# Attention's work on TensorE in four blocks a batch by how it uses the array, with the other engines' order redrawn

## The chip, the cores and the metric

The kernel runs on one core of one Trainium2 chip. The metric is the device time of one execution in microseconds; several executions give a median. The core has five engines that matter here, each of which works through its own list of instructions in order and waits for others at semaphores: TensorE (PE in the profile), VectorE (DVE), ScalarE (ACT), GpSimd (POOL) and SyncE (SP, which only issues transfers).

## The reference, cut to what matters

2048 tokens (8 batches of 256) with 128 features go through two layers, each of them a mixing part and a feed-forward part, with a residual and a layer norm behind each. The change touches only the third part, a linear attention with exponential feature maps:

```python
qkv = x @ Wqkv + bqkv                       # 16 heads of 8
def _feature_map(t, omega):                 # 32 features a head
    return jnp.exp(einsum('bhnd,dm->bhnm', t, omega) - 0.5 * sum(t * t, -1))
k_sum = jnp.sum(k_prime, axis=2)
denominator = einsum('bhnm,bhm->bhn', q_prime, k_sum)[..., None]
k_v = einsum('bhnm,bhnd->bhmd', k_prime, v)
numerator = einsum('bhnm,bhmd->bhnd', q_prime, k_v)
out = numerator / (denominator + 1e-06)
return out @ Wout + bout
# around it: x = _layernorm(x + attention(x))
```

(The reference calls it with four batches of 512 in mind, but here its input has eight batches of 256.) Ahead of it stand a gated convolution and a mixture of eight experts, behind it a gated MLP with two square layers.

## The kernel before, in words

Every engine's list is written out by hand. In attention each engine works in steps `s`; `attention(step, first, end)` calls `attention_step(s)` for each. One call handles several batches at once, at different stages: `values(s - 2)` is batch `s - 2`, and a call for a batch that doesn't exist does nothing. Semaphores count up by batch; `wait(engine, sem, n)` waits only where `n > 0`. A batch `b` goes through these stages:

- GpSimd `answers_sum` (L603) and `x2_residual` (L609) add the experts' two answers and the kept row. For batches 4 to 7 the answers come from HBM late. VectorE `x2_moments` (L962, L970) takes mean and variance, GpSimd `x2_root` (L477, L480) the inverse root, VectorE `x2_norm` (L987) normalises.
- TensorE `x2_transposes` (L1990) turns the rows; ScalarE `turned_x2` copies them out twice; GpSimd `low_x2` (L616) makes the low part.
- TensorE `keys_or_queries(b, 0)` makes keys, `(b, 1)` queries (three products each, L1695 to L1697); ScalarE `biased_and_squared` writes them and their squares. TensorE `values` (L2001), VectorE `biased_v` (L1483).
- TensorE `key_features` (L2026) and then, in the same PSUM room, `query_features` (L2035); ScalarE `key_exps` (L831) and `query_exps` (L837).
- TensorE `key_sums` (L2048); VectorE `own_sums` (L1492, L1495) transposes and masks them; TensorE `query_products` (L2065, L2062) makes numerator and denominator.
- VectorE `inverse_sums` (L1504, a reciprocal) and `attended` (L1510); TensorE `attention_rows` (L2076, L2077); VectorE `x3_residual` (L1517) and `x3_moments`; GpSimd `x3_root`; VectorE `x3_norm` (L987); TensorE `x3_transposes` (L2086); ScalarE `high_x3` and VectorE `low_x3` (L1532) split it for the MLP.

TensorE addresses its array in three ways here, which the profile shows as contraction rows * output columns: the full array (128*128: transposes, keys, queries, values, rows out), 32 rows (32*128: the two feature maps, four products side by side) and 32 columns (128*32: key sums and query products, again four side by side). The step of before goes through them as values | query features | x2 transposes, queries | key sums | key features | rows out, x3 transposes, keys | query products: seven changes a step.

VectorE's step in before, in order, is `biased_v(s-3)`, `inverse_sums(s-5)`, `attended(s-5)`, `own_sums(s-4)`, `x3_norm(s-6)`, `x3_residual(s-5)`, `x2_moments(s)`, `x2_norm(s-1)`, `low_x3(s-6)`, `x3_moments(s-5)`. `x3_residual(b)` waits for `attention_rows(b)`; `values(b)` waits for the transpose in `own_sums(b-2)`, which frees its half of PSUM bank 2. After the last step VectorE goes on with the MLP's gating (L1554).

## Time and profile before

| | us |
|---|---|
| median of 3 runs | 332.81 |
| lowest, highest | 332.07, 333.74 |
| span of the profiled execution | 343.1 |
| TensorE busy | 313.5 (91%) |
| VectorE busy | 249.8 (73%) |
| ScalarE busy | 189.2 (55%) |
| GpSimd busy | 161.4 (47%) |

The profiled execution is 10.3 us longer than the median: the times of the rows are those of that execution, and a difference worked out from them is set against its 343.1. Busy is the time in which an engine has an instruction under way. Consecutive instructions overlap at their ends, so that what an instruction costs in a full engine is read from its start to the next one's start, not from its duration. The chain that ended last runs 54% on TensorE and 14% on VectorE over the whole span. Attention lies between about 185 and 243 us.

### The profile page before, as it was taken

What the parts mean: (1) busy time and instruction counts of PE and PEld (TensorE: products, weight loads), DVE (VectorE), ACT (ScalarE), POOL (GpSimd) and SP (SyncE); (2) the same over time, 40 slices, a digit from 0 to 9 for tenths busy, and PEclk for the clock granted to TensorE, in tenths of its full rate; (3) what the DMA queues carried; (4) which work ended last, traced back from release to release, by engine and by line L of the source; (5) the groups of instructions that cost most, each with busy time, mean ns of one, the idle gap of its engine ahead of it and who ended that gap; (6) DMA issues with size and microseconds to landing.
All of it is one profiled execution on the core that took longest, in us unless ns stands there. A gap on an engine that the chain in (4) does not pass through costs nothing.

```text
span 343.1 us, 8922 instructions
## 1 busy us (share of the span) xinstructions
PE 313.5 (91%) x2917; PEld 283.8 (83%) x2917; DVE 249.8 (73%) x852; ACT 189.2 (55%) x401; POOL 161.4 (47%) x221
## 2 busy tenths in 40 slices
PE   7999999988893699999999999999889999999993
PEld 4988988978782599999888776776678999999993
DVE  2577988878890348968985589878995787667844
ACT  3144886654450246646547655654657766767333
POOL 1014577867777445698588584221130433144200
PEclk9999999999998589999999999999999999999998
DMA  6991011122133432522430400000000000000001
GB/s 207 418 403 67 16 34 33 33 54 48 49 71 93 152 111 71 186 63 65 115 96 32 129 14 2 2 3 4 1 2 0 3 15 18 15 15 0 16 18 34
DMA packets 17051, 23.22 MB, mean 68 GB/s; under 512 B 3440, under 2 KB 14448, under 8 KB 16224
## 3 DMA queue, kind: packets, MB, share of 16 engines
q1 hardware_dynamic: 14016, 17.84, 16.3%
q0 software_dynamic: 2272, 4.69, 4.1%
q8 instruction: 24, 0.39, 0.5%
q10 hardware_dynamic: 720, 0.14, 0.2%
q14 instruction: 19, 0.16, 0.1%
HBM read 16.93 MB, written 6.73 MB: 69 GB/s over the span
## 4 chain that ended last, share of the span: by engine, by line
PE 54%; DVE 14%; another core or an unknown queue 4%; issue 4%; ACT 3%; POOL 2%; DVEq 0%; POOLq 0%; ACTq 0%
PE ps L2104 9%; PE ps L2105 9%; PE ps L1931 6%; PE ps L1695 3%; PE ps L1697 3%; PE ps L1917 3%; PE ps L2168 3%; PE ps L1696 3%; PE ps L2026 3%; PE ps L2035 2%; PE ps L2048 2%; PE ps L2065 1%; DVE sb_work L1504 1%; PE ps L1891 1%
## 5 line engine op out<-in xcount | busy, mean ns | idle before, releaser
L2104 PE MATMUL ps<-sb_w_hi,sb_fh_hi 128*128 128x256 f32 x256 | 61.2, 283 | 1.2 <-DVE sb_w_lo L957 0.6
L2105 PE MATMUL ps<-sb_w_lo,sb_fh_hi 128*128 128x256 f32 x256 | 59.9, 278 | 0.0
L2104 PEld LDWEIGHTS ps<-sb_w_hi,sb_fh_hi 128*128 128x128 f32 x256 | 48.2, 188 | 2.4 <-issue 1.1
L2105 PEld LDWEIGHTS ps<-sb_w_lo,sb_fh_hi 128*128 128x128 f32 x256 | 48.2, 188 | 0.0
L1931 PE MATMUL ps<-sb_w,sb_stage 128*128 x234 | 34.6, 286 | 4.6 <-issue 4.6
L493 POOL DMA_INDIRECT routed<-sb_rows_of,sb_row x32 | 32.0, 999 | 11.8 <-issue 8.7
L1931 PEld LDWEIGHTS ps<-sb_w,sb_stage 128*128 128x128 f32 x234 | 30.9, 201 | 5.0 <-issue 4.8
L643 POOL TENSOR_TENSOR sb_w_lo<-sb_x_in,sb_w_hi 128x256 fp32r<-128x256 f32 x24 | 17.5, 754 | 34.9 <-DVE sb_w_hi L1627 34.9
L477 POOL TENSOR_TENSOR sb_veps_h<-sb_mv_h,sb_eps 128x2 f32<-128x2 f32 x16 | 5.1, 318 | 54.5 <-DVE sb_mv_h L970 48.9
L1695 PE MATMUL ps<-sb_w_hi,sb_rT_hi 128*128 x78 | 29.3, 375 | 0.4 <-ACT sb_stage L771 0.4
L595 POOL DMA_INDIRECT answers<-sb_stage x24 | 24.1, 1004 | 11.0 <-ACT sb_stage L777 7.1
L1697 PE MATMUL ps<-sb_w_hi,sb_rT_lo 128*128 x78 | 25.9, 332 | 0.0
L1696 PE MATMUL ps<-sb_w_lo,sb_rT_hi 128*128 x78 | 25.8, 330 | 0.0
L1917 PE MATMUL ps<-sb_const,sb_stage 128*128 128x128 f32 x117 | 20.1, 281 | 4.3 <-ACT sb_stage L783 3.1
L1695 PE MATMUL ps<-sb_front_hi,sb_xT_hi 128*128 128x512 f32 (+1 forms) x64 | 23.2, 362 | 0.7 <-DVE sb_xT_lo L1004 0.7
L595 POOL DMA_INDIRECT answers<-sb_xT_in x15 | 14.4, 960 | 13.9 <-ACT sb_xT_in L777 9.0
L882 ACT ACTIVATE sb_xT_in<-ps,sb_ff_s 128x256 f32<-128x256 f32 x32 | 14.5, 474 | 11.5 <-PE ps L2105 9.0
L874 ACT ACTIVATE sb_work<-ps,sb_ff_s 128x256 f32<-128x256 f32 x32 | 13.9, 474 | 12.5 <-PE ps L2105 12.5
L1696 PE MATMUL ps<-sb_front_lo,sb_xT_hi 128*128 128x512 f32 (+1 forms) x64 | 20.5, 320 | 0.0
L1697 PE MATMUL ps<-sb_front_hi,sb_xT_lo 128*128 128x512 f32 (+1 forms) x64 | 20.5, 320 | 0.0
L1917 PEld LDWEIGHTS ps<-sb_const,sb_stage 128*128 128x128 f32 x117 | 14.6, 144 | 6.3 <-issue 4.0
L891 ACT ACTIVATE sb_x_in<-ps,sb_ff_s 128x256 f32<-128x256 f32 x32 | 14.2, 477 | 9.3 <-PE ps L2105 9.3
(307 smaller groups left out, 928.6 us busy)
## 6 DMA issues: line engine op xcount, KB each, us to landing
sb_stage<-in_w SPq DMA_DIRECT2D x2, 1408.0 KB, 13.9
sb_stage<-routed SPq DMA_DIRECT2D x24, 65.0 KB
sb_w<-in_w SPq DMA_DIRECT2D x1, 1536.0 KB, 18.6
sb_x_in<-in_x_tok SPq DMA_DIRECT2D x1, 1024.0 KB, 9.6
sb_x_in<-in_ff_h SPq DMA_DIRECT2D x1, 1024.0 KB
sb_xT_in<-in_ff_h SPq DMA_DIRECT2D x1, 1024.0 KB
sb_got_first<-answers SPq DMA_DIRECT2D x4, 256.0 KB, 3.4
sb_w<-answers SPq DMA_DIRECT2D x4, 256.0 KB, 4.1
```

The lines of the kernel that those rows point to most:

```text
L493: nc.gpsimd.indirect_dma_start(routed[:, :], bass.IndirectOffsetOnAxis(ap=row[:, b, r:r + 1], axis=0), rows_of[:, b, r, :], None).then_inc ...
L595: nc.gpsimd.indirect_dma_start(answers[:, :], bass.IndirectOffsetOnAxis(ap=routed_row(t)[:, AT_DEST:AT_DEST + 1].bitcast(u32), axis=0), ro ...
L643: nc.gpsimd.tensor_tensor(a_lo[:, m, :], f_a[:, m, :], a_hi[:, m, :].bitcast(fp32), ALU.subtract).then_inc(ff["a_lo"], 1)
L882: nc.scalar.activation(f_last[:, m, :], half_bank(6, m), ACT.Gelu, scale=ff_s[:, 3, m:m + 1]).then_inc(ff["g2"], 1)
L891: nc.scalar.activation(f_g[:, m, :], second_bank(b, m), ACT.Gelu, scale=ff_s[:, 2, m:m + 1]).then_inc(ff["g1"], 1)
L1695: mm(dst, lhs[0], rhs[0], start=start, stop=False)
L1696: mm(dst, lhs[0], rhs[1], start=False, stop=False)
L1697: return mm(dst, lhs[1], rhs[0], start=False, stop=stop)
L1917: last = transpose(ps[:, 1, k * P:(k + 1) * P], hid[:, u % FLY, k * P:(k + 1) * P], ident)
L1931: last = mm(ps[:, down_bank(u), 0:D], hidT[:, u % FLY, k * P:(k + 1) * P], w2[:, e, k, :], start=k == 0, stop=k == HIDDEN_TILES - 1)
L2104: mm(dst, w_hi, x_hi, start=start, stop=False)
L2105: last = mm(dst, w_hi, x_lo, start=False, stop=stop and exact)
```

## The change

TensorE's step is put in the order key features (32 rows) | keys, queries, values, x2 transposes, rows out, x3 transposes (full array) | query features (32 rows) | query products, key sums (32 columns): four changes a step. Keys and queries of a batch stand behind each other and wait for both of the batch before. The queries' exponentials get a second buffer, `qp_of`, in room that the experts' part has left free, so that they wait for the query products of two batches before. The `attention_step` of ScalarE, VectorE and GpSimd is written anew to this order, and one batch more of the work before the features is in flight. The work itself, its instructions and their sizes, stay as they are.

```diff
-        qp = act1_room[:, 0:HEAD_GROUPS * SEQ].rearrange("p (g t) -> p g t", t=SEQ)
+        qp_of = [r[:, 0:HEAD_GROUPS * SEQ].rearrange("p (g t) -> p g t", t=SEQ) for r in (act1_room, hid_room)]
 # GpSimd
             def attention_step(s):
-                answers_sum(s)
-                x3_root(s - 6)
-                x2_root(s - 1)
-                low_x2(s - 2)
-                x2_residual(s)
+                answers_sum(s + 1)
+                x2_residual(s + 1)
+                x3_root(s - 4)
+                low_x2(s)
+                x2_root(s + 1)
...
                 x2_root(3)
-                answers_sum(4)
-                x2_residual(4)
-                low_x2(3)
-                x2_root(4)
-                answers_sum(5)
-                x2_residual(5)
...
-            attention(attention_step, first=6, end=ATTENTION_STEPS + 1)
+            attention(attention_step, first=3, end=ATTENTION_STEPS - 1)
 # ScalarE
-                    act.wait_ge(at["qk"], 2 * b + part + 1)
+                    act.wait_ge(at["qk"], 2 * b + (part + 1 if b == 0 else 2))
...
-                    wait(act, at["nd"], b)
-                    nc.scalar.activation(qp[:, :, :], features, ACT.Exp).then_inc(at["qp"], 1)
+                    wait(act, at["nd"], b - 1)
+                    nc.scalar.activation(qp_of[b % 2], features, ACT.Exp).then_inc(at["qp"], 1)
...
                     act.wait_ge(at["tr"], b + 1)
+                    wait(act, at["tr3"], b - 4)
...
             def attention_step(s):
-                query_exps(s - 3)
-                turned_x2(s - 1)
-                biased_and_squared(s - 2, 1)
                 key_exps(s - 2)
+                biased_and_squared(s - 1, 0)
+                turned_x2(s)
                 high_x3(s - 5)
-                biased_and_squared(s - 1, 0)
+                query_exps(s - 2)
+                biased_and_squared(s - 1, 1)
...
-            attention(attention_step, first=4, end=ATTENTION_STEPS - 1)
+            attention(attention_step, first=2, end=ATTENTION_STEPS - 1)
 # VectorE
             def attention_step(s):
-                biased_v(s - 3)
-                inverse_sums(s - 5)
-                attended(s - 5)
-                own_sums(s - 4)
-                x3_norm(s - 6)
-                if s < ATTENTION_STEPS:
-                    x3_residual(s - 5)
-                x2_moments(s)
-                x2_norm(s - 1)
-                if s < ATTENTION_STEPS:
-                    low_x3(s - 6)
-                    x3_moments(s - 5)
+                own_sums(s - 3)
+                x2_norm(s)
+                biased_v(s - 1)
+                x3_residual(s - 4)
+                x3_moments(s - 4)
+                x2_moments(s + 1)
+                low_x3(s - 5)
+                x3_norm(s - 4)
+                inverse_sums(s - 3)
+                attended(s - 3)
...
-            attention(attention_step, first=6, end=ATTENTION_STEPS + 1)
+            attention(attention_step, first=3, end=ATTENTION_STEPS - 1)
 # TensorE
-                    wait(pe, at["x3_lo"], b - 4)
+                    wait(pe, at["x3_lo"], b - 5)
...
-                    wait(pe, at["st"], 2 * b + part)
+                    wait(pe, at["st"], 2 * b)
...
             def attention_step(s):
-                values(s - 2)
-                query_features(s - 3)
-                x2_transposes(s - 1)
-                keys_or_queries(s - 2, 1)
-                key_sums(s - 3)
                 key_features(s - 2)
+                keys_or_queries(s - 1, 0)
+                keys_or_queries(s - 1, 1)
+                values(s - 1)
+                x2_transposes(s)
                 attention_rows(s - 4)
                 x3_transposes(s - 5)
-                keys_or_queries(s - 1, 0)
+                query_features(s - 2)
                 query_products(s - 3)
+                key_sums(s - 2)
...
             keys_or_queries(1, 0)
+            keys_or_queries(1, 1)
             values(1)
+            x2_transposes(2)
             query_features(0)
-            x2_transposes(2)
-            keys_or_queries(1, 1)
             odd_weights()
             key_sums(0)
-            key_features(1)
-            keys_or_queries(2, 0)
-            query_products(0)
-            attention(attention_step, first=4, end=ATTENTION_STEPS - 1)
+            attention(attention_step, first=3, end=ATTENTION_STEPS - 1)
```

The calls that ScalarE and VectorE made by hand ahead of their steps for the same batches go away with it.

## Rows read from the trace of the kernel before

**Rows 1.** Busy time by stretch: us, then busy us (instructions) by engine; attention's stretch

```profile
185.00:243.00 58.00, 54.94 (x939) 40.99 (x940) 46.24 (x139) 34.42 (x65) 24.79 (x42) 1.00 0.08 24
```

**Rows 2.** Timeline of TensorE, one steady step: start us, us, engine, line, instructions

```profile
216.11 0.71 PE L2001 MATMUL ps<-sb_wv,sb_work 128*128 128x128 f32 x4
216.75 1.15 PE L2035 MATMUL ps<-sb_x_in,sb_omega 32*128 32x256 f32 x16
217.83 0.44 PE L1990 MATMUL ps<-sb_const,sb_rows_of 128*128 128x128 f32 x2
218.03 0.36 PE L1695 MATMUL ps<-sb_xT_hi,sb_qk_hi 128*128 128x256 f32 x1
...
218.55 1.08 PE L2048 MATMUL ps<-sb_stage,sb_xT_in 128*32 128x128 f32 x32
219.56 1.17 PE L2026 MATMUL ps<-sb_omega,sb_x_in 32*128 32x128 f32 x32
220.67 0.23 PE L2076 MATMUL ps<-sb_bout,sb_ones_bf 128*128 128x128 bf16 x1
...
222.12 0.64 PE L2065 MATMUL ps<-sb_stage,sb_hT 128*32 128x256 f32 x8
...
223.22 0.71 PE L2001 MATMUL ps<-sb_wv,sb_work 128*128 128x128 f32 x4
```

**Rows 3.** Timeline of TensorE before the steady steps, values behind a full-array product

```profile
186.56 0.61 PE L2001 MATMUL ps<-sb_wv,sb_work 128*128 128x128 f32 x4
```

**Rows 4.** Timeline of VectorE over the steady step

```profile
216.33 0.48 DVE L962 BATCH_NORM_STATS2 sb_stats_h<-sb_stage 128x6 f32<-128x128 f32 x2
...
217.12 0.46 DVE L1483 TENSOR_TENSOR sb_xT_in<-ps,sb_bv 128x128 f32<-128x128 f32 x2
217.50 1.75 DVE L1504 RECIPROCAL sb_work<-ps 128x256 f32<-128x256 f32 x1
219.28 0.42 DVE L1510 TENSOR_TENSOR sb_work<-ps,sb_work 128x256 f32<-128x256 f32 x1
219.70 0.45 DVE L1492 STREAM_TRANSPOSE sb_hT<-ps 128x256 f32<-128x256 f32 x1
220.18 0.31 DVE L1495 TENSOR_TENSOR sb_hT<-sb_hT,sb_const 128x128 f32<-128x128 f32 x1
220.42 0.60 DVE L987 SCALAR_TENSOR_TENSOR sb_rows_of<-sb_stage,sb_mv_h,sb_rstd_hs 128x128 f32<-128x128 f32 x2
221.54 0.42 DVE L1517 TENSOR_TENSOR sb_stage<-ps,sb_rows_of 128x256 f32<-128x256 f32 x1 [0.52 <-PE ps L2077]
221.88 0.60 DVE L987 SCALAR_TENSOR_TENSOR sb_rows_of<-sb_work,sb_mv_odd,sb_rstd_odd 128x128 f32<-128x128 f32 x2
222.41 0.42 DVE L1532 TENSOR_TENSOR sb_w_lo<-ps,sb_w_hi 128x256 fp32r<-128x256 f32 x1
```

**Rows 5.** Timeline of GpSimd over the steady step

```profile
217.29 0.19 POOL L477 TENSOR_TENSOR sb_veps_h<-sb_mv_h,sb_eps 128x2 f32<-128x2 f32 x1 [3.47 <-DVE sb_mv_h L970]
217.56 0.71 POOL L480 TENSOR_TENSOR sb_rstd_hs<-sb_veps_h,sb_minus_half 128x2 f32<-128x2 f32 x1
...
219.62 0.73 POOL L616 TENSOR_TENSOR sb_xT_lo<-sb_work,sb_xT_hi 128x256 fp32r<-128x256 f32 x1 [0.41 <-ACT sb_work L846]
```

**Rows 6.** Timeline of GpSimd, the two sums of batch 4

```profile
195.34 0.73 POOL L603 TENSOR_TENSOR sb_work<-sb_w 128x256 f32<-128x256 f32 x1 [3.21 <-DMA sb_w<-answers]
196.14 0.73 POOL L609 TENSOR_TENSOR sb_res<-sb_work,sb_rows_of 128x256 f32<-128x256 f32 x1
```

**Rows 7.** The reciprocals' line: durations ns min/median/max, first and last start

```profile
L1504 DVE RECIPROCAL sb_work<-ps x8: 1726/1748/1757, 194.9 to 242.9; 128x256 f32<-128x256 f32 x8
```

**Rows 8.** Timeline of VectorE, the first product of the MLP's gating

```profile
245.54 0.87 DVE L1554 SCALAR_TENSOR_TENSOR sb_x_in<-ps,sb_ff_s,sb_work 128x256 f32<-128x256 f32 x2
```

**Rows 9.** Timeline of VectorE, the product over GpSimd's addition

```profile
205.12 0.83 DVE L1495 TENSOR_TENSOR sb_hT<-sb_hT,sb_const 128x128 f32<-128x128 f32 x1
```

**Rows 10.** Timeline of GpSimd, that addition

```profile
205.07 0.73 POOL L609 TENSOR_TENSOR sb_res<-sb_work,sb_rows_of 128x256 f32<-128x256 f32 x1
```

More of the change, by code:

```diff
@@ L910, in _ @@
             biased_and_squared(0, 1)
-            key_exps(0)
-            biased_and_squared(1, 0)
-            query_exps(0)
-            turned_x2(2)
-            biased_and_squared(1, 1)
-            key_exps(1)
-            biased_and_squared(2, 0)
-            attention(attention_step, first=4, end=ATTENTION_STEPS - 1)
+            attention(attention_step, first=2, end=ATTENTION_STEPS - 1)
             nc.scalar.activation(touched[:, :], ones[:, 0:1], ACT.Silu)
@@ L1652, in _ @@
             odd_count()
-            own_sums(0)
-            x2_norm(3)
-            biased_v(2)
-            inverse_sums(0)
-            attended(0)
-            x2_moments(4)
-            own_sums(1)
-            x3_residual(0)
-            x2_norm(4)
-            x2_moments(5)
-            x3_moments(0)
-            attention(attention_step, first=6, end=ATTENTION_STEPS + 1)
+            attention(attention_step, first=3, end=ATTENTION_STEPS - 1)
             mlp_first(0, (0, 1))
@@ L2065, in query_products @@
                             last = mm(ps[32 * g:32 * g + 32, 3, a * SEQ:(a + 1) * SEQ], sums,
-                                      qp[:, g, :], start=a == 0, stop=True)
+                                      qp_of[b % 2][:, g, :], start=a == 0, stop=True)
                     last.then_inc(at["nd"], 1)
```

## Prediction, made before the changed kernel was run

> **What bounds the kernel now.** I read the page's slices for the stages, then busy time by stretch, then the timeline of each engine over one steady step of attention. In attention TensorE is busy 54.9 of 58.0 us and VectorE 46.2 [rows 1]. The reader should then see that a steady step lasts 223.22 - 216.11 = 7.11 us, from one `values` to the next, and that TensorE has no hole in it [rows 2]. In the same step VectorE once waits for TensorE, 0.52 us before `x3_residual` [rows 4]. So TensorE's own order sets the pace, and VectorE is close behind. How close is the question of this change, since it both shortens TensorE's step and redraws VectorE's.
>
> **TensorE's own step.** Seven changes of array shape become four. What one costs is seen in the same four products `values`: 0.71 us behind query products of 128*32 [rows 2], 0.61 behind full-array products [rows 3], so 0.1 within the group; the drain ahead of the group is not isolated by any row, and I bound it by 0 and 0.1 more. Three changes fewer are 0.3 to 0.6 us a step, so TensorE's step would be 6.5 to 6.8 us. I take 6.65. The TensorEngine Tiling page of the Trainium skill (Tiling Modes, Key Properties) says that changing the mode drains the engine, which these rows bear out in direction.
>
> **VectorE's own step.** From start to start [rows 4]: reciprocal 1.78 (217.50 to 219.28), `attended` 0.42, `own_sums` 0.72 (219.70 to 220.42), a norm 0.53 (221.88 to 222.41) twice, `x3_residual` 0.34, moments 0.79 (216.33 to 217.12) twice, `biased_v` 0.38, and `low_x3` at most its duration, 0.42. Sum: 1.78 + 0.42 + 0.72 + 1.06 + 0.34 + 1.58 + 0.38 + 0.42 = 6.70 us. That is already TensorE's new step, before a single wait. The same page (PSUM Bottleneck) says that a faster TensorE doesn't speed up the evacuation of PSUM, which may then be the bound.
>
> **The loop in the new order.** VectorE's new step is own sums, x2 norm, biased v, x3 residual, x3 moments, x2 moments, low x3, x3 norm, reciprocal, attended. Two of its neighbours are on a loop that passes through other engines. First, `attention_rows(s-4)` stands behind `x2_transposes(s)` in TensorE's list, and those wait for `x2_norm(s)`, which VectorE does only after `attended(s-4)` and `own_sums(s-3)`. In before, the rows could go as soon as `attended` was done. Second, the x3 norm now stands ahead of the next reciprocal and waits for GpSimd's root of moments taken just before; in before the root had the whole reciprocal as cover. One turn, from a reciprocal to the next, is then:
>
> - reciprocal 1.78, `attended` 0.42, `own_sums` 0.72, x2 norm 0.60 to its end [rows 4]: 3.52
> - hand-over to TensorE 0.05; no row isolates it, the nearest bounds it by 0 and 0.17 (the last moments' next instruction starts at 217.12 and GpSimd's answer to them at 217.29 [rows 4, 5]); I take a value low in this, since it appears twice a turn. Sum 3.57
> - x2 transposes to the next group 0.20 (217.83 to 218.03) [rows 2]: 3.77
> - rows out, from their start to `x3_residual`'s 0.87 (220.67 to 221.54) [rows 2, 4]: 4.64. `biased_v` fits in here at no cost
> - `x3_residual` 0.34: 4.98
> - start of moments to end of root 1.94 (216.33 to 217.56 + 0.71) [rows 4, 5], hand-over 0.05: 6.97. x2 moments and low x3 (0.79 + 0.42, behind 0.79) end at 6.98, so they are just hidden in it, and where there are none the wait is the same
> - x3 norm 0.53: 7.50.
>
> So a full turn takes 7.50 us against 7.11 before. TensorE needs 6.65 of it and waits the rest, at the x2 transposes. With the hand-overs at their bounds it is 7.40 to 7.74.
>
> **The start.** Batch 4's answers land late: GpSimd waits 3.21 us for them and ends the sum at 196.14 + 0.73 = 196.87 [rows 6]. That transfer is issued by SyncE behind the experts' stores, which nothing here moves, so I leave it there. In the new order `x2_moments(4)` stands ahead of the first reciprocal, and that is queued behind it: 196.87 + 0.05 + 0.79 = 197.71, against 194.9 in before [rows 7]. `attended(0)` is queued behind that, and the rows of batch 0 behind both.
>
> **The sum.** Reciprocals, by batch: 0 at 197.71; 1 to 4 at 7.50 each: 205.21, 212.71, 220.21, 227.71. For batch 5 there are no x2 transposes left, but `values(7)` waits for the transpose of `own_sums(5)`: 1.78 + 0.42 + 0.45 + 0.05 = 2.70, values 0.45 (0.61 from rows 3, less the overlap at its end, an estimate between 0.4 and 0.6), then 0.87 + 0.34 + 1.99 + 0.53: 6.88, 234.59. For batches 6 and 7 the rows go straight behind `attended`: 1.78 + 0.42 + 0.05 + 0.87 + 0.34 + 1.99 + 0.53 = 5.98 each: 240.57, 246.55, against 242.9 in before [rows 7]. VectorE's first product of the MLP follows 2.20 later, at 248.75 against 245.54 [rows 8]: +3.2, and `x3_residual(7)` two products on waits 0.1 for its rows. From there on VectorE and TensorE feed each other as in before, with the same lists, so nothing gives the delay back. 343.1 + 3.3 = 346.4 in the profiled execution; the median of 332.81 is 0.97 of that span, and 3.3 x 0.97 = 3.2 gives 336.0 us.
>
> **Edits that I cost at nothing.** The second buffer for the queries' exponentials frees ScalarE from waiting for the query products of the batch before; ScalarE is busy 34.4 of 58.0 us [rows 1], and behind query features TensorE now has query products and key sums, two groups of about a microsecond, before it needs the PSUM room again. Without the buffer the exponentials would wait for the very query products behind them: about 1 us a step. ScalarE's new wait for the x3 transposes (`tr3`) holds the copy of x2 and what is queued behind it, `high_x3` and the queries' exponentials; the query features that these need come after the x3 transposes anyway. Joining keys and queries moves the wait for both earlier squares ahead by one group; they are written 2 us before. GpSimd's sums for the next batch now run at the head of its step, under VectorE's reciprocal, which reads PSUM; only if they run on into `own_sums` do they cost what the next part prices.
>
> **The rivals.**
> - TensorE stays the bound, as the new order would have it. For this VectorE would have to be free of the loop, with turns of 6.65 for the five with x2 work; the two last ones as in before. Before took 242.9 - 194.9 = 48.0 us from first to last reciprocal [rows 7]. If the first one stays put, five turns save 0.46 each and the shorter start 1 us: -3.3, 329.6 us. For it: TensorE's step has no hole now [rows 2]. Against: the loop above is in the order itself.
> - No change that can be told. If batch 4's answers land 2 us sooner (less of the 3.21 wait), or the start's later groups, which are done ahead in the new order, shorten what follows, the start costs 0.8 instead of 2.8: 334.0 us, and within 0.5% with a little luck in the turns. For it: only the start carries 2.8 of the 3.3.
> - Slower still, by the port between VectorE and GpSimd. VectorE's product took 0.83 us where it met GpSimd's addition [rows 9, 10] and 0.31 where it met GpSimd's `low_x2` [rows 4, 5]. In the new order `low_x2` starts together with the x3 norm, as both follow the root. By the row the norm isn't slowed. If it is, it waits 0.73 - 0.05 each in four turns: +2.7, 338.7 us. The page SBUF - State Buffer of the Trainium skill (SBUF: two separate sides) says that a VectorE instruction with two SBUF inputs and a GpSimd one that reads SBUF exclude each other; by that rule, this rival holds, and the row of 0.31 us speaks against it.
>
> **How the numbers follow.** The loop with the late start 0.55 (336.0, itself 334.5 to 337.5 by hand-overs and start), no difference 0.22, TensorE's pace 0.16, the port 0.07. A measurement of this kernel tells 0.5% (1.7 us) from no change. Slower 0.62, same 0.22, faster 0.16. The range reaches from near the second rival's other side, 330.0, to the port's, 338.6.
>
> **What would show it.** Right: reciprocals of batches 1 to 4 some 7.5 us apart; TensorE idle 0.5 to 1 us each step ahead of L1990, ended by VectorE's L987; VectorE idle ahead of the x3 norm, ended by GpSimd's L480; the first reciprocal after 197. Wrong: a step below 7 us with no hole in TensorE (the first rival), the first reciprocal near 195 (the second), an x3 norm over 1 us long (the third). The likeliest error is in the loop: a hand-over or a group that I put behind another although it was ready.

## The result and the profile after

| | before | after |
|---|---|---|
| median of 4 runs, us | 332.44 | 338.00 |
| lowest, highest, us | 332.05, 333.74 | 336.38, 340.50 |
| span of the profiled execution, us | 343.1 | 335.7 |

After takes 1.0186 of the time of before, 95% interval 1.0131 to 1.0242: slower by 4.4 to 8.0 us, where 3.2 was forecast. This ratio, like those below, is worked out from the undisturbed runs of both kernels, so it need not be the ratio of the two medians, which is 1.0167 here. The two profiled spans can't be set against each other: that of before had a granted clock of 0.90 in the 70 us before 170, that of after 1.00. So attention is compared from its first key features on, at 185.00 in before and at 170.55 in after. The work just ahead of it is the same: from the last longer wait of TensorE (0.61 us) to the first key features it is 4.78 us in both.

From the page of after: the span, TensorE's granted clock by slice (in tenths), and the chain that ended last, by engine.

```profile
span 335.7 us, 8921 instructions
...
PEclk9999999999999999999999799999999999999998
...
PE 40%; DVE 20%; issue 9%; POOL 8%; DMA 2%; ACT 1%; DVEq 0%; SPq 0%; POOLq 0%
```

The chain runs 20% on VectorE and 8% on GpSimd. In before it was 54% TensorE and 14% VectorE. One slice of the clock shows a 7: it covers 184.6 to 193.0 us, early in attention.

Attention's stretch again, from the first key features to the last reciprocal (it answers to rows 1), and the reciprocals' line (rows 7) and the first product of the MLP's gating (rows 8).

```profile
170.55:235.44 64.89, 55.51 (x947) 43.16 (x948) 47.38 (x141) 34.70 (x66) 25.54 (x44) 0.97 0.07 21
```

```profile
L1492 DVE RECIPROCAL sb_work<-ps x8: 1723/1744/1752, 183.1 to 235.4; 128x256 f32<-128x256 f32 x8
```

```profile
237.56 0.87 DVE L1540 SCALAR_TENSOR_TENSOR sb_x_in<-ps,sb_ff_s,sb_work 128x256 f32<-128x256 f32 x2
```

The stretch is 64.9 us long instead of 57.9, with nearly the same instructions in it: TensorE is busy 55.5 us of it (54.9 before), VectorE 47.4 (46.2), and the rest is waiting. From first to last reciprocal it is 52.4 us against 48.0 [rows 7], and the gating begins 67.01 behind the first key features against 60.54 [rows 8]: +6.5, which stays until the end (+7.0).

One full turn of the loop, on VectorE (answers to rows 4), TensorE (rows 2) and GpSimd (rows 5): start, duration, engine, line, then the idle time just before and what ended it.

```profile
191.97 1.74 DVE L1492 RECIPROCAL sb_work<-ps 128x256 f32<-128x256 f32 x1
...
194.09 0.44 DVE L1480 STREAM_TRANSPOSE sb_hT<-ps 128x256 f32<-128x256 f32 x1
...
194.77 0.61 DVE L975 SCALAR_TENSOR_TENSOR sb_rows_of<-sb_work,sb_mv_odd,sb_rstd_odd 128x128 f32<-128x128 f32 x2
...
196.57 0.43 DVE L1505 TENSOR_TENSOR sb_stage<-ps,sb_rows_of 128x256 f32<-128x256 f32 x1 [0.69 <-PE ps L2052]
197.03 0.49 DVE L950 BATCH_NORM_STATS2 sb_stats_h<-sb_stage 128x6 f32<-128x128 f32 x2
...
199.02 1.09 DVE L975 SCALAR_TENSOR_TENSOR sb_rows_of<-sb_stage,sb_mv_h,sb_rstd_hs 128x128 f32<-128x128 f32 x2
200.03 1.74 DVE L1492 RECIPROCAL sb_work<-ps 128x256 f32<-128x256 f32 x1
```

```profile
194.67 0.68 PE L1976 MATMUL ps<-sb_wv,sb_work 128*128 128x128 f32 x4 [0.68 <-DVE sb_hT L1480]
195.43 0.44 PE L1965 MATMUL ps<-sb_const,sb_rows_of 128*128 128x128 f32 x2
```

```profile
198.28 0.71 POOL L480 TENSOR_TENSOR sb_rstd_hs<-sb_veps_h,sb_minus_half 128x2 f32<-128x2 f32 x1
198.96 0.74 POOL L616 TENSOR_TENSOR sb_xT_lo<-sb_work,sb_xT_hi 128x256 fp32r<-128x256 f32 x1
```

The turn takes 200.03 - 191.97 = 8.06 us. TensorE, which had no hole in before, idles 0.68 ahead of `values` until `own_sums` has its transpose (0.91 in the next three turns); VectorE idles 0.69 for the rows out. And the x3 norm at 199.02 takes 1.09 us, where it took 0.60 in rows 4. It starts while GpSimd's `low_x2` runs (198.96, 0.74). In before, too, there was such a norm, in the turn ahead of that of rows 4, beside an addition of GpSimd's (VectorE, then GpSimd):

```profile
213.15 1.08 DVE L987 SCALAR_TENSOR_TENSOR sb_rows_of<-sb_stage,sb_mv_h,sb_rstd_hs 128x128 f32<-128x128 f32 x2
```

```profile
213.04 0.78 POOL L609 TENSOR_TENSOR sb_work<-sb_work,sb_rows_of 128x256 f32<-128x256 f32 x1
```

The reciprocals of after, one to the next, are 8.91, 8.06, 8.06, 8.06, 7.06, 6.11 and 6.11 us apart. Forecast: 7.50 four times, 6.88, 5.98 twice. In before they are 7.59, 7.70, 7.28, 6.88, 7.11, 5.91 and 5.51 apart, so that before's turns, too, are not all 7.11. The list of after, and the delay of the first reciprocal behind the first key features, are what the experiments are compared by. They repeat closely from trace to trace (12 below), while the times of one kernel scatter by several us.

### The profile page after: what moved, and what is told of

Its sections match the earlier page's. It is cut to its first block, busy times and chain, and to the rows that moved or that the text cites. A ratio compares the mean times of both kernels' runs of the same rounds, so it can differ in the third digit from the quotient of the medians.

```text
span 335.7 us, 8921 instructions
## 1 busy us (share of the span) xinstructions
PE 304.6 (91%) x2917; PEld 278.6 (83%) x2917; DVE 250.1 (75%) x852; ACT 189.6 (56%) x401; POOL 161.6 (48%) x221
## 4 chain that ended last, share of the span: by engine, by line
PE 40%; DVE 20%; issue 9%; POOL 8%; DMA 2%; ACT 1%; DVEq 0%; SPq 0%; POOLq 0%
PE ps L2079 9%; PE ps L2080 9%; PE ps L1906 4%; DVE sb_work L1492 4%; PE ps L2143 3%; PE ps L1670 2%; PE ps L1672 2%; POOL answers L595 2%; PE ps L1671 2%; PE ps L1892 2%; DMA routed<-sb_rows_of,sb_row 2%; PE ps L2052 2%; DVE sb_rows_of L975 1%; DVE sb_stats_h L950 1%; POOL sb_work L603 1%
## 5 line engine op out<-in xcount | busy, mean ns | idle before, releaser
L1906 PE MATMUL ps<-sb_w,sb_stage 128*128 x234 | 32.7, 276 | 0.0
L1906 PEld LDWEIGHTS ps<-sb_w,sb_stage 128*128 128x128 f32 x234 | 29.2, 192 | 0.1
L1670 PE MATMUL ps<-sb_w_hi,sb_rT_hi 128*128 x78 | 28.4, 364 | 0.2 <-ACT sb_stage L765 0.2
L1672 PE MATMUL ps<-sb_w_hi,sb_rT_lo 128*128 x78 | 25.2, 323 | 0.0
L1671 PE MATMUL ps<-sb_w_lo,sb_rT_hi 128*128 x78 | 25.1, 321 | 0.0
L1670 PE MATMUL ps<-sb_front_hi,sb_xT_hi 128*128 128x512 f32 (+1 forms) x64 | 22.4, 350 | 0.8 <-DVE sb_xT_lo L992 0.8
L1892 PE MATMUL ps<-sb_const,sb_stage 128*128 128x128 f32 x117 | 19.3, 273 | 1.2 <-DVE sb_stage L1365 1.2
L1671 PE MATMUL ps<-sb_front_lo,sb_xT_hi 128*128 128x512 f32 (+1 forms) x64 | 19.8, 309 | 0.0
L765 ACT ACTIVATE sb_stage<-ps,sb_stage 128x352 f32<-128x352 f32 x24 | 13.3, 555 | 11.1 <-PE ps L1672 10.2
L1358 DVE SCALAR_TENSOR_TENSOR sb_stage<-ps,sb_stage 128x352 f32<-128x352 f32 x24 | 14.0, 583 | 6.9 <-ACT sb_stage L765 6.6
```

The source lines that it names most:

```text
L1670: mm(dst, lhs[0], rhs[0], start=start, stop=False)
L1671: mm(dst, lhs[0], rhs[1], start=False, stop=False)
L1672: return mm(dst, lhs[1], rhs[0], start=False, stop=stop)
L1892: last = transpose(ps[:, 1, k * P:(k + 1) * P], hid[:, u % FLY, k * P:(k + 1) * P], ident)
L1906: last = mm(ps[:, down_bank(u), 0:D], hidT[:, u % FLY, k * P:(k + 1) * P], w2[:, e, k, :], start=k == 0, stop=k == HIDDEN_TILES - 1)
```

## The experiments

Four things were open: why a turn has 0.56 more than forecast, why the first has 1.41 more, what the late start is worth, and where TensorE's gain from grouping went. Below, "turns" are the distances from one reciprocal to the next, and "gating" is the start of the MLP's gating behind the first key features. Ratios are to before, run beside it on the same chip, with a 95% interval.

### 1. low_x2 away from the x3 norm

```diff
                 x3_root(s - 4)
-                low_x2(s)
                 x2_root(s + 1)
+                low_x2(s)
```

> One edit to the changed kernel: in GpSimd's step x2_root(s + 1) stands ahead of low_x2(s), so that low_x2 no longer starts together with VectorE's x3 norm. The changed kernel's x3 norm takes 1.08 us where it meets low_x2 (four turns) and 0.61 where it doesn't. Theory of the port: all x3 norms take 0.6, the four turns become 7.6 instead of 8.06 us, the time falls by 1.9 us to about 336.2 (ratio to before about 1.013). Rival, that the norm is long for another reason, such as the root's result arriving: the norm stays at 1.08 and the time at 338.

VectorE and GpSimd over the step in which the norm follows GpSimd's root:

```profile
200.75 0.61 DVE L975 SCALAR_TENSOR_TENSOR sb_rows_of<-sb_stage,sb_mv_h,sb_rstd_hs 128x128 f32<-128x128 f32 x2
201.28 1.75 DVE L1492 RECIPROCAL sb_work<-ps 128x256 f32<-128x256 f32 x1
...
208.33 0.61 DVE L975 SCALAR_TENSOR_TENSOR sb_rows_of<-sb_stage,sb_mv_h,sb_rstd_hs 128x128 f32<-128x128 f32 x2
208.86 1.75 DVE L1492 RECIPROCAL sb_work<-ps 128x256 f32<-128x256 f32 x1
```

```profile
200.01 0.70 POOL L480 TENSOR_TENSOR sb_rstd_hs<-sb_veps_h,sb_minus_half 128x2 f32<-128x2 f32 x1
...
200.96 0.70 POOL L480 TENSOR_TENSOR sb_rstd<-sb_veps,sb_minus_half 128x2 f32<-128x2 f32 x1
201.62 0.74 POOL L616 TENSOR_TENSOR sb_xT_lo<-sb_work,sb_xT_hi 128x256 fp32r<-128x256 f32 x1
```

Ratio 1.0228 (1.0150 to 1.0306), turns 9.87, 7.59, 7.58, 8.05, 7.06, 6.11, 6.11. With `low_x2` at 201.62 the norm is back at 0.61 us, and the next turn takes 208.86 - 201.28 = 7.58, within 0.1 of the forecast 7.50. In the fourth turn there is no x2 root to lie between them, the two meet again (1.08), and the turn is 8.05. So the norm's 0.47 and the turn's 0.47 come and go together: the collision is shown as the cause. The total didn't come down, since the first turn took 9.87. In that turn the edit had a price of its own: `low_x2(3)` now stood behind the root of batch 4, which waits for the late sums, and TensorE waited for it ahead of the keys. The line of that wait, and where the clock stood behind it (stretch, us, then each engine's busy us, then the granted clock):

```profile
185.71 0.38 PE L1670 MATMUL ps<-sb_xT_hi,sb_qk_hi 128*128 128x256 f32 x1 [2.06 <-POOL sb_xT_lo L616]
```

```profile
187.00:193.00 6.00, 5.96 (x44) 3.93 (x46) 3.57 (x15) 2.51 (x6) 1.94 (x5) 0.50 0.01 3
```

TensorE ran at 0.50, its lower level of 1.2 GHz, until 193.3. After had 0.50 only until 189.4. The first turn is 0.96 longer than in after; the later `low_x2`, an x2 norm of 1.08 us beside an addition (0.61 in after) and the longer stretch at 0.50 all lie in it. No run isolates their shares, but in experiment 6, with the first two as here and the clock back by 192.4, the first turn is 8.12; experiment 3's edit, which is in it too, is worth 0.5 of the difference. So the clock has the larger part.

### 2. The late sums' moments behind the reciprocal

```diff
-                x2_moments(s + 1)
+                if s != 3:
+                    x2_moments(s + 1)
 ...
                 attended(s - 3)
+                if s == 3:
+                    x2_moments(s + 1)
```

> One edit to the changed kernel: in step 3 alone VectorE takes the moments of batch 4, which wait for late answers, after the first reciprocal and attended instead of ahead of them. Theory that the start costs 2.5 us by this queueing, and that TensorE's 1.8 us of idle time behind it also let the granted clock fall (0.55 and 0.69 in the groups behind it): first reciprocal 2 us earlier, no stretch under 1.00 in attention, first turn 8.1 instead of 8.9 us, time lower by 2.5 to 3 us, about 335.3. Rival, that the start is given back later since x2 of batch 4 is then late: first turn longer by what the start gained, time within 0.7 us of 338.

VectorE, then TensorE, in the first turn:

```profile
183.28 1.76 DVE L1492 RECIPROCAL sb_work<-ps 128x256 f32<-128x256 f32 x1 [1.95 <-PE ps L2043]
...
187.38 1.61 DVE L975 SCALAR_TENSOR_TENSOR sb_rows_of<-sb_res,sb_mv,sb_rstd 128x128 f32<-128x128 f32 x2 [0.40 <-POOL sb_rstd L480]
```

```profile
189.05 0.69 PE L1968 MATMUL ps<-sb_const,sb_rows_of 128*128 128x128 f32 x2 [1.60 <-DVE sb_rows_of L975]
```

Ratio 1.0276 (1.0169 to 1.0382). The first reciprocal came 10.57 us behind the key features instead of 12.50, as meant, and the first turn then took 11.91 instead of 8.91. The x2 norm of batch 4 now fell beside GpSimd's two additions for batch 5 and took 1.61 us, and TensorE idled 1.60 for it and had a clock of 0.50 from 188.3 to 195.2. The first reciprocal alone is no lever: its turn still needs batch 4's x2, which came no sooner. What the late start costs by itself stays open, as the slowed norm and the clock came with the edit.

### 3. The rows out ahead of the x2 transposes

```diff
-                x2_transposes(s)
                 attention_rows(s - 4)
+                x2_transposes(s)
```

> One edit to the changed kernel: on TensorE attention_rows(s - 4) stands ahead of x2_transposes(s), so that the rows no longer wait for x2_norm(s). Theory of the loop: x3_residual starts 4.05 us behind the reciprocal's start instead of 4.60, the four turns with x2 work shorten by 0.55 each, time lower by 2.2 us, about 335.8. Rival, that VectorE's own work sets the turn: biased_v and the residual only change places in time, turns stay at 8.06 and the time at 338.

Ratio 1.0186 (1.0114 to 1.0258), turns 9.67, 7.56, 7.55, 7.53, then as after. Each full turn is 0.50 shorter with the norm still at 1.08, so TensorE's order, the rows behind the x2 transposes, costs 0.5 us a turn by itself. The first turn grew by 0.76, with the clock at 0.50 from 186.5 to 193.3, so the total again showed nothing. The wait ahead of `values` was 1.81 us, as in after (1.82), where the clock was back by 189.4: how long it stays low differs behind the same wait.

### 4. The reciprocal ahead of the x3 norm

```diff
-                x3_norm(s - 4)
                 inverse_sums(s - 3)
                 attended(s - 3)
+                x3_norm(s - 4)
```

> One edit to the changed kernel: on VectorE inverse_sums and attended stand ahead of x3_norm(s - 4), so that GpSimd's root has the reciprocal as cover. Theory of the loop: no idle time ahead of the x3 norm; the turns with x2 work fall from 8.06 to 7.5 (to 8.0 if the norm now meets GpSimd's additions at the port), the three last ones from 6.11 to about 5.5, time lower by 2 to 4 us, 334 to 336. Rival, that TensorE is the bound after all: turns unchanged.

```profile
194.01 1.10 DVE L975 SCALAR_TENSOR_TENSOR sb_rows_of<-sb_stage,sb_mv_h,sb_rstd_hs 128x128 f32<-128x128 f32 x2
195.03 0.44 DVE L1480 STREAM_TRANSPOSE sb_hT<-ps 128x256 f32<-128x256 f32 x1
```

Ratio 1.0144 (1.0086 to 1.0202), turns 8.08, 8.07, 8.11, 7.58, 7.06, 5.58, 5.14. The root's latency is covered, as in before, but the norm at 194.01 (1.10) now meets GpSimd's additions and stands in front of `own_sums`, for which TensorE waits. The full turns stayed at 8.07 to 8.11; the first (8.08 instead of 8.91), the fourth (7.58) and the last two became shorter (gating +65.0 instead of +67.0). In the full turns the cover was given back to the same contention.

### 5. TensorE kept busy through the wait

Sixteen products whose results nobody reads, put between the queries and `values` of the step in which batch 4 is awaited:

```diff
                 keys_or_queries(s - 1, 1)
+                if s == 4:
+                    spare_products(0, 16)
                 values(s - 1)
```

> One edit to the changed kernel: in step 4 TensorE runs 16 spare products of 256 columns (about 1.8 us, results unused, extra work) while it would otherwise stand idle ahead of values(3). Theory that the idle time there lets the granted clock fall and so lengthens the first turn: granted clock 1.00 through attention, first turn near 8.1 instead of 8.9 to 9.9 us, the later turns as in the changed kernel (8.06 three times), R7 about 1 us earlier. Rival, that the first turn is long because of the order alone: it stays at 8.9 or more.

Of after, TensorE's waits and its clock around that place (columns: stretch, us, then busy us and instructions of TensorE, its weight loads, VectorE, ScalarE, GpSimd, then the granted clock):

```profile
185.74 0.97 PE L1976 MATMUL ps<-sb_wv,sb_work 128*128 128x128 f32 x4 [1.82 <-DVE sb_hT L1480]
```

```profile
185.70:188.40 2.70, 2.66 (x12) 2.26 (x12) 1.23 (x5) 0.66 (x2) 0.01 (x1) 0.55 0.00 0
188.40:190.00 1.60, 1.60 (x21) 1.12 (x24) 1.30 (x7) 0.00 (x0) 0.06 (x1) 0.69 0.00 0
190.00:194.00 4.00, 4.00 (x94) 3.11 (x90) 3.48 (x8) 2.59 (x4) 3.76 (x7) 1.00 0.01 4
```

Of the experiment:

```profile
183.60 1.95 PE L1677 MATMUL ps<-sb_ones_bf 128*128 128x256 bf16 x16
```

```profile
182.00:191.00 9.00, 8.88 (x150) 6.96 (x147) 7.32 (x24) 4.23 (x8) 5.00 (x11) 1.00 0.04 13
```

In after TensorE idled 1.82 us ahead of `values`, and then had a granted clock of 0.55 and 0.69 for 4.3 us: the lower of its two levels, 1.2 of 2.4 GHz, for most of it. The same four products took 0.97 instead of 0.68 us. With the spare products the clock stayed at 1.00, and the first turn took 8.04 instead of 8.91. Ratio 1.0156 (1.0076 to 1.0235); the total gained 0.8 (66.19 to the gating instead of 67.01). The spare products are the only edit, so the clock's share is shown: 0.87 us.

### 6. Experiments 1 and 3 together

```diff
-                low_x2(s)
                 x2_root(s + 1)
+                low_x2(s)
...
-                x2_transposes(s)
                 attention_rows(s - 4)
+                x2_transposes(s)
```

> The two edits of rows_before_x2 and port_apart together. By the loop they add up, since they cut different pieces of one turn: turns with x2 work 7.55 - 0.5 = 7.1 us where the norm is 0.6 us long, which is the pace of the kernel before. Rival: with both pieces gone another wait (the root, or the transpose that values wait for) keeps the turn at 7.5.

Ratio 1.0098 (1.0055 to 1.0141), turns 8.12, 7.07, 7.07, 7.53, 7.06, 6.11, 6.1; gating +63.8. The two gains add: 8.06 - 0.5 - 0.49 = 7.07. In the full turns this is below before's 7.70 and 7.28, but the start (+12.6 to the first reciprocal, +9.9 in before), the fourth turn, in which the norm is slowed again, and the last two (6.11, in before 5.91 and 5.51) cost more than that. As in experiment 1, TensorE waited ahead of the first turn's keys (2.05), and the clock was at 0.50, here from 188.9 to 192.4.

### 7. The four blocks, with VectorE's order of before

TensorE's step keeps the four blocks but has the rows ahead of `values` and the x3 transposes ahead of x2's; VectorE has the x3 norm of the step before behind `own_sums`, so that the root is covered by the reciprocal; GpSimd lets batch 5's additions wait until batch 4's x2 is written; the late moments stand behind the reciprocal. Only lines of the steps are shown:

```diff
 (VectorE)
+                x3_norm(s - 5)
                 x2_norm(s)
                 biased_v(s - 1)
...
-                x2_moments(s + 1)
+                if s != 3:
+                    x2_moments(s + 1)
...
-                x3_norm(s - 4)
...
+                if s == 3:
+                    x2_moments(s + 1)
 (TensorE)
+                attention_rows(s - 4)
                 values(s - 1)
+                x3_transposes(s - 5)
                 x2_transposes(s)
-                attention_rows(s - 4)
-                x3_transposes(s - 5)
 (GpSimd)
+                if s == 4:
+                    pool.wait_ge(at["x2"], 5)
                 answers_sum(s + 1)
```

> The changed kernel with VectorE's order laid as before's around the norm: own_sums(s - 3), x3_norm(s - 5), x2_norm(s), biased_v, x3_residual, x3_moments, x2_moments(s + 1), low_x3, inverse_sums, attended; rows ahead of values and x3 transposes ahead of x2's on TensorE; in step 3 the reciprocal ahead of batch 4's moments, and GpSimd's additions for batch 5 behind x2_norm(4). Theory that TensorE's four groups are worth 0.5 us a step once the loop is gone: turns with x2 work 6.6 to 6.9 us, TensorE without holes in steps 5 to 7, first product of the MLP 58 to 60 us behind the first key features (before 60.5, changed kernel 67.0), time 1 to 2 us below before. Rival, that VectorE's own work (6.7 us) and its small waits leave nothing: turns 7.1, time equal to before.

VectorE over one turn:

```profile
198.19 1.76 DVE L1494 RECIPROCAL sb_work<-ps 128x256 f32<-128x256 f32 x1
199.99 0.42 DVE L1500 TENSOR_TENSOR sb_work<-ps,sb_work 128x256 f32<-128x256 f32 x1
...
200.80 0.65 DVE L1485 TENSOR_TENSOR sb_hT<-sb_hT,sb_const 128x128 f32<-128x128 f32 x1
201.37 0.60 DVE L977 SCALAR_TENSOR_TENSOR sb_rows_of<-sb_stage,sb_mv_h,sb_rstd_hs 128x128 f32<-128x128 f32 x2
...
202.82 0.41 DVE L1507 TENSOR_TENSOR sb_stage<-ps,sb_rows_of 128x256 f32<-128x256 f32 x1
203.27 0.48 DVE L952 BATCH_NORM_STATS2 sb_stats_h<-sb_stage 128x6 f32<-128x128 f32 x2
...
205.25 1.76 DVE L1494 RECIPROCAL sb_work<-ps 128x256 f32<-128x256 f32 x1
```

12 runs, ratio 0.9991 (0.9952 to 1.0030): as fast as before. Turns 7.47, 7.07, 7.06, 6.69, 6.41, 6.17, 5.85; gating +59.9. `x3_residual` at 202.82 has no idle time ahead of it any more: VectorE goes from one reciprocal to the next without waiting for another engine, in 7.06 us. In this turn the loop is gone and VectorE is the bound. From the fourth turn on VectorE waits for TensorE's query products again (0.66, 0.38, 0.95 and 0.64 us). From first to last reciprocal it is 46.7 us, against 48.0 in before: 1.3 us less, of which 0.6 went to the first reciprocal, which came at +10.5 instead of +9.9. Whether the 1.3 us are the grouping's or come from fewer collisions with GpSimd is not told apart. Ahead of the gating the clock stood at 0.50 from 229.2 to 232.6, behind a wait of 1.47; what that cost is not shown. The forecast's sum for VectorE was 6.70. From start to start in these rows, `attended` and `own_sums` take 1.38 together (199.99 to 201.37) instead of 1.14, as the product at 200.80 (0.65) meets GpSimd's addition, and `x3_residual` 0.45 instead of 0.34: that is 0.35 of the 0.36 between.

### 8. Before again

> The kernel before, unchanged, for a second trace. The first one had a granted clock of 0.963 ahead of attention and a span of 343.1 us. If that is what made its span 10 us longer than the median time, this one spans about 331 us, with attention from first key features to first product of the MLP unchanged at 60.5 us (also the noise of such a stretch). If attention itself differs by over 1 us, stretches of single traces can't be compared so finely.

A single run of 333.19 us, span 331.4, clock 0.98 from 100 to 170, first reciprocal +9.31, turns 8.09, 7.51, 7.28, 6.88, 7.11, 5.91, 5.51, gating +60.22. The 343.1 us span of the first profile was that one execution, whose clock ahead of attention was low; attention as a whole is within 0.3 us of it, its first reciprocal and first turn differ by 0.6 and 0.5 and make up for each other.

### 9. and 10. Before and the blocks of 7, each with half of the reciprocal

Both kernels take the reciprocal over the first 128 columns only, so the second half of the sums isn't inverted and that part of the output is not computed. It makes VectorE's step some 0.8 us shorter, so that TensorE's own step can show.

```diff
-                    V.reciprocal(rden, ps[:, 3, SEQ:])
+                    V.reciprocal(rden[:, 0:P], ps[:, 3, SEQ:SEQ + P])
```

> The kernel before with each attention reciprocal halved: it is taken over 128 of 256 columns, the other half of the quotients uses old values (work left out). VectorE's turn loses 0.87 us. Theory that in before TensorE's seven changes of shape set the pace: the steady turns stay at 6.9 to 7.1 us.

> The kernel before_order (four groups on TensorE, VectorE's order as in before) with the same half of each reciprocal left out. Theory that TensorE's grouped step is worth 0.4 to 0.5 us, and was hidden under VectorE's 7.06: the turns with x2 work fall to 6.6 us, against 7.0 for before_cut. Rival, that the grouping is worth next to nothing: both stand at 7.0.

TensorE in before with the cut, `values` at the head of each step:

```profile
202.45 0.71 PE L2001 MATMUL ps<-sb_wv,sb_work 128*128 128x128 f32 x4
...
209.56 0.71 PE L2001 MATMUL ps<-sb_wv,sb_work 128*128 128x128 f32 x4
...
216.67 0.71 PE L2001 MATMUL ps<-sb_wv,sb_work 128*128 128x128 f32 x4
```

In the grouped order with the cut, the key features that begin a step, and VectorE's wait in the last of them:

```profile
198.37 1.17 PE L2007 MATMUL ps<-sb_omega,sb_x_in 32*128 32x128 f32 x32
...
205.14 1.17 PE L2007 MATMUL ps<-sb_omega,sb_x_in 32*128 32x128 f32 x32
...
211.77 1.17 PE L2007 MATMUL ps<-sb_omega,sb_x_in 32*128 32x128 f32 x32
```

```profile
211.04 0.96 DVE L1494 RECIPROCAL sb_work<-ps 128x128 f32<-128x128 f32 x1 [0.60 <-PE ps L2046]
```

Before's later steps are 7.28, 7.11, 7.11 as without the cut: there a VectorE that is 0.8 us a step faster gives nothing, so TensorE was the bound, as the forecast said (in the 7.28, with or without the cut, some 0.2 are a wait for a slowed norm of 1.08). The step ahead of them was not TensorE's alone: it took 7.96 in before, with TensorE idle 0.72 ahead of the x3 transposes for a norm that GpSimd's additions had slowed (1.07), and 7.44 with the cut. The grouped steps are 6.95, 6.77, 6.63. In the first two TensorE still waits a little for VectorE's x2 norm (its transposes at 194.92 and 201.71 follow the norm's end at 194.86 and 201.65); in the last VectorE waits 0.60 for TensorE (L2046). So 6.63 is the grouped step of TensorE by itself, 0.48 less than 7.11; the forecast had 6.65. The other pairs of steps differ by 0.33 and 0.34. With the whole reciprocal VectorE's 7.06 hides this gain in the full turns. A single run each: 330.92 and 329.29 us.

### 11. The x2 norm on GpSimd

Kernel 7 with the x2 norms of batches 4 to 7 done by GpSimd, behind the root, to take 0.53 off VectorE. GpSimd's first addition for the batch after the next follows them, and its second waits for `biased_v`. The diff is against kernel 7 and shows lines of the steps only:

```diff
 (GpSimd)
-                if s == 4:
-                    pool.wait_ge(at["x2"], 5)
-                answers_sum(s + 1)
+                if s < BATCHES - 1:
+                    pool.wait_ge(at["v_tok"], s)
                 x2_residual(s + 1)
...
+                if s + 1 >= 4:
+                    x2_norm(s + 1)
+                answers_sum(s + 2)
 (VectorE)
-                x2_norm(s)
+                if s < 4:
+                    x2_norm(s)
```

> before_order with x2_norm of batches 4 to 7 moved from VectorE to GpSimd, right behind the root and under the reciprocal, and GpSimd's additions split so that the second starts behind biased_v. VectorE's turn loses 0.53 for the norm and 0.35 that own_sums lost at the port: 7.06 - 0.88 = 6.2, so that TensorE's 6.6 us becomes the bound. Theory: turns with x2 work 6.6 to 6.8 us, first product of the MLP 58 to 59 us behind the first key features (before 60.2 to 60.5), time 1 to 2 us under before. Rival, that the port gives GpSimd's norm no cheaper place: turns 7.0 or more, time as before.

```profile
185.21 1.58 POOL L626 TENSOR_SCALAR sb_rows_of<-sb_res,sb_mv,sb_rstd 128x128 f32<-128x128 f32 x2
```

```profile
186.85 0.44 PE L1984 MATMUL ps<-sb_const,sb_rows_of 128*128 128x128 f32 x2 [1.65 <-POOL sb_rows_of L626]
```

12 runs, ratio 1.0032 (0.9989 to 1.0074), turns 8.51, 6.89, 7.05, 6.62, 6.41, 6.17, 6.34. GpSimd takes 1.58 us for what costs VectorE 0.53. The x2 of batch 4 came later and TensorE idled 1.65 for it, this time with the clock at 1.00 behind it; the x3 norm then met the end of GpSimd's norm and the addition behind it (1.11, 1.13), which took back what VectorE had been relieved of.

### 12. After again

> The changed kernel, unchanged, on the chip of these runs. The ratio to before is again 1.015 to 1.020; first product of the MLP 66 to 68 us behind the first key features; turns with x2 work 8.06, the first one 8.1 to 9.9 by how far the granted clock falls in it.

Ratio 1.0210 (1.0132 to 1.0287). Turns 8.91, 8.07, 8.07, 8.05, 7.05, 6.12, 6.11: the same to 0.02, the first among them.

## Where the prediction failed, and what it had right

The direction and the loop were right: TensorE stopped being the bound, a loop through VectorE, TensorE and GpSimd took its place, and the time got longer. The size was not: the ratio of 1.0186 on the 332.81 from which the forecast set out is 339.0, above the 336.0 of the forecast and just above the range's upper end of 338.6; the median, compared with a before of 332.44, is 338.0. The step that failed is "By the row the norm isn't slowed": it put the collision of VectorE's norm with GpSimd at nothing, and it measured 0.47 us in each of four turns. Two smaller terms add to it, `x3_residual` (0.12 short in each turn) and the clock, which had no term (0.87 once). Step by step, with times behind the first key features:

- **What bounds the kernel before.** TensorE: confirmed by `before_cut` for the steady steps. In the step from 200.88 to 208.84, ahead of the one that the forecast read, TensorE waited 0.72 for VectorE.
- **TensorE's own step**, 6.65: 6.63 in `grouped_cut`.
- **The start.** The first reciprocal was forecast at 197.71 - 185.00 = +12.71 and came at +12.50, behind the late sums:

```profile
182.25 0.48 DVE L950 BATCH_NORM_STATS2 sb_stats<-sb_res 128x6 f32<-128x128 f32 x2 [3.09 <-POOL sb_res L609]
...
183.05 1.72 DVE L1492 RECIPROCAL sb_work<-ps 128x256 f32<-128x256 f32 x1
```

  That it costs what it was delayed by is not shown: `moments_late` freed it without a gain.
- **The loop**, 7.50 a turn: 7.59 where the norm isn't disturbed (`port_apart`). The place of TensorE's wait was wrong. I had it at the x2 transposes; the trace has it one group earlier, at `values` (0.68), which wait for `own_sums`' transpose, and the x2 transposes follow the norm at once (195.38 to 195.43). The wait that the forecast gave as a sign, 0.5 to 1 us ahead of L1990, is therefore not there. The one of VectorE ahead of the x3 norm, ended by L480, is there in the turns without x2 moments (0.78), and in the others it is hidden, as the sum had it. The length is forecast all the same: the term of `x3_residual` below was 0.12 short and the others 0.03 long together.
- **"By the row the norm isn't slowed"**: this step failed. The x3 norm took 1.08 to 1.09 instead of 0.61 in four turns, 4 x 0.47 = 1.9 us. The row of 0.31 was misread. In rows 4 and 5 `low_x2` runs from 219.62 to 220.35 and the product starts at 220.18: it overlapped the last 0.17 us only, and lost 0.02 by it (0.31 against 0.29 where it met nothing). It was no row for two instructions that start together, and such a row, 9 over 10, stood beside it with 0.83. The same x3 norm stood slowed in the trace of before as well: 1.08 beside the addition at 213.04, shown above, and 1.07 at 205.88, so its price could have been read there. I gave this 0.07. The page SBUF - State Buffer of the Trainium skill (SBUF: two separate sides) says that the two exclude each other; here the trace agrees, with 0.47 us, and the forecast had set the misread row above it. The rival's price, 0.68 each, was too high; measured it is 0.47. GpSimd's record runs 0.68 past the start of the norm (199.02 to 199.70), yet the norm lost 0.47. Both rows fit a hold that ends some 0.2 us ahead of the record's end, but no run isolated that.
- **"`x3_residual` 0.34"**: this term was too small. 0.34 is the distance to an instruction that doesn't need its result. The moments do, and start 0.46 behind it (196.57 to 197.03). 7 x 0.12 = 0.8 us, in all turns, and it makes most of the tail turns' 6.11 instead of 5.98.
- **The granted clock** had no term in "The start". Behind the wait for batch 4 it fell to 0.55 and then 0.69, and the first turn took 0.87 more (`kept_busy`).
- **The rivals.** TensorE's pace is excluded by its 0.7 to 0.9 us of idle time in each full turn, no difference by the interval. The port is what came true, by the sign given for it, an x3 norm over 1 us long. Its 338.7 was the loop's 336.0 plus 2.7. That 338.0 is so near it is in part luck: its price was 0.8 too high in all, and the terms of `x3_residual` and the clock, 1.7 together, were missing.
- **The sum.** From first to last reciprocal 52.38 instead of 48.84: 3.54 more, of which 1.9 + 0.8 + 0.9 = 3.6 are named above. The first reciprocal and the way to the gating were 0.2 and 0.1 shorter, so the gating came 6.5 later than in before, not 3.2.
- **"The median is 0.97 of that span"**: this took one execution's low clock in an earlier stage for a property of the kernel. It made 0.1 us here.
- **VectorE's own step**, 6.70: 7.06 in `before_order`. The same two faults make the difference, an own result waited for (0.11) and an addition of GpSimd's met (0.33, less 0.09 by which the term of `attended` was too long).
- **The edits costed at nothing.** ScalarE ended none of the waits in a full turn's rows. What the second buffer alone is worth was not tried.

Where the gain went: TensorE's grouped step is up to 0.48 us shorter, but in the full turns of `before_order` VectorE needs 7.06 us against TensorE's 7.11 before. Of these 7.06, 0.33 are a collision with an addition of GpSimd's; whether an order can avoid it without a price elsewhere was not shown. The Trainium skill's page TensorEngine Tiling (Array Packing) (PSUM Bottleneck) says that tiling makes TensorE faster but not the emptying of PSUM, which may become the bound. 7 against 10 agrees in direction, 7.06 with the whole reciprocal and 6.77 with half of it, though VectorE's step here is norms and moments as well. None of the versions run was faster than before beyond its interval; `before_order` (0.9952 to 1.0030) equals it. Taking a norm off VectorE and giving it to GpSimd brought nothing (11).

## What to carry to other kernels

Before the busiest engine is made faster, add up the second engine's step from start to start. Where the sum comes within a few per cent, as here, little of the gain may arrive, and a new order can add waits of its own. Where two instructions are to be priced together, look for a row in which they start together, check in both timelines how much of them overlapped, and read every occurrence of the instruction, not only that of one step. After each new wait on TensorE, read the clock of the stretch behind it: the wait may be paid twice.

## What the runs showed of the hardware

- A two-half norm on VectorE (0.61 us, each half some 0.3) took 1.08 when an elementwise instruction of GpSimd's on 128x256 (0.74) started just before it, and 1.61 across two such instructions. GpSimd's kept their 0.73 to 0.74 in after; where the norm had started first, one took longer: 0.85 at 205.95 in before, beside the norm of 205.88. Its roots on 128x2 tiles disturbed nothing: with one beside it the norm stayed at 0.61 (200.75 over 200.96 in `port_apart`). VectorE's reciprocal from PSUM took 1.72 to 1.76 whatever GpSimd did.
- Behind `x3_residual` an instruction of VectorE that reads its result started 0.12 us later (0.46, in after) than one that doesn't (0.34, in before).
- The granted clock doesn't follow from the length of an idle time alone. Behind 1.82 us of it (after) it was at 0.50 from 186.0 to 189.4, behind 1.81 (`rows_before_x2`) from 186.5 to 193.3, behind 1.65 (`norm_on_gpsimd`) it stayed at 1.00. The rows out of batch 6 came behind the same wait (2.00 and 1.99) in two traces, and the clock from 2 to 3 us later on was 1.00 in after and 0.50 in `port_apart`:

```profile
231.60:235.00 3.40, 2.84 (x33) 2.03 (x34) 2.15 (x9) 1.87 (x3) 0.89 (x2) 1.00 0.00 0
```

```profile
234.50:237.00 2.50, 2.50 (x19) 1.69 (x12) 1.73 (x6) 0.83 (x2) 0.89 (x2) 0.50 0.00 0
```

  There it cost nothing, since VectorE sets the last turns (6.11 in both). The waits of 0.7 to 0.9 us ahead of `values` in the full turns left the clock at 1.00 in every trace.
- The same norm took GpSimd, as a TENSOR_SCALAR, 0.79 us a tile, and VectorE, as a SCALAR_TENSOR_TENSOR, 0.27 to 0.30.
